# Attention exponentials read from PSUM with a bias, in a recurrent kernel whose four engines wait on one another

## The chip, the cores and the metric

The kernel runs on one core of a Trainium2 chip. The metric is the device time of one execution in microseconds, lower is better. The engines are called PE (TensorE), DVE (VectorE), ACT (ScalarE), POOL (GpSimd) and SP; each runs its own queue of instructions in order, and semaphores are the only thing that ties one queue to another.

## The reference, cut to what matters

An LSTM runs over 128 time steps of 16 sequences, its outputs go through a causal attention with 16 heads of 64 (keys and values from a 32-wide latent), the result is added to x and goes through a GRU of 128 steps, and a mixture of 8 experts (top 2) follows. The part that is changed is the softmax:

```python
attn = jnp.einsum('bqhd,bkhd->bhqk', q_blhd, k_blhd) / jnp.sqrt(HD)
attn = jax.nn.softmax(jnp.where(mask, attn, neg_inf), axis=-1)
y_blhd = jnp.einsum('bhqk,bkhd->bqhd', attn, v_blhd)
```

## The kernel before, in words

All stages are staggered over one loop of steps k. The LSTM's time step t = k runs in step k, the GRU's time step g = k - 29 in the same step, so that both recurrences advance once a step, and every engine has the same loop with its own part of the step written out by hand. Nothing is scheduled by a tool: the order in the code is the order in each queue.

The attention works on blocks of 16 queries. Write a step as k = 16q + o, where o is its offset in block q (1 to 8). Eight *units* belong to a block, one for each offset 2 to 9. A unit holds two sequences with 16 heads and 16 queries each, which makes four tiles of 128 rows; the keys are the L = 16q positions so far. For unit n:

- step of its scores (offset o): PE writes the four tiles, 128 x L each, into the single PSUM bank `pS` (`scores`, L493 to L500); DVE takes the row maxima `mx` (`maximum`, L858) and writes `P = pS - mx` for all four tiles in one instruction (`subtract`, L867). The bank is free for the next writer once `sub_done` has counted.
- next step: ACT takes the exponential of `P` in place, four tiles in one instruction (`exps`, L730), PE transposes the four tiles into `pV` (`turn_probs`, L507), ACT copies them out (L736).
- step after that: PE multiplies by the latents (`values`), DVE normalises (`normalise`, `turn_values`).

`P` has three buffers, `mx` has one. `pS` is also the bank into which the latents are projected every eighth step (`lat_q`).

Within a step the queues are, in order. PE: `g_step` (GRU gates), `l_step` (LSTM gates), `values`, `g_candidate` (the matmul of the GRU's candidate, pG<-gRZ), `lat_q` if due, `scores`, one expert's down projection (pY), `turn_probs`, then what is due of the router, the fills of pL and pG and the propagation. ACT: `gT` (tanh of the GRU's gates), `lT` (tanh of the LSTM's gates), `exps` of the unit before, `gC` (tanh of the candidate), `lC`, then the rest. DVE: `gRZ` (L949, releases `g_candidate`), the LSTM's cell, `normalise`, `gB`, `ghi`, `g`, then `glo` (L973, released to the next `g_step`), `hhi`, `hlo`, then `maximum`, `subtract`, at offset 6 the second half of a router's work (`route_rest`), the expert's accumulation `acc` (L940), `turn_values`, and at offset 5 the first half (`route_first`), which ends in `low`; ACT's `th` (L778) waits for `low` and stands ahead of the next step's `gT`.

The experts' Gelu (L746) runs at offsets 13 to 15, 0 and 1; from block 3 on this puts an `ACT_TABLE_LOAD` ahead of the first exponential of a block, at offset 3. It happens six times.

Of the kernel before, what the change touches and what calls it, by code (L numbers as in the profile page):

```python
# [15 lines left out]
NU = B // 2  # L16
# [8 lines left out]
O_S, O_T, O_V = 2, 3, 4  # L25
# [9 lines left out]
def unit_at(k, o):  # L35
    q, u = divmod(k - o, TB)
    return NU * (q - 1) + u if u < NU and 1 <= q <= NBLK else None
# [42 lines left out]
def build(nc, a, out):  # L80
# [3 lines left out]
    ALU = mybir.AluOpType  # L84
    ACT = mybir.ActivationFunctionType
    AX = mybir.AxisListType

    ctx = ExitStack()
    with ctx:
# [6 lines left out]
        def sem(name):  # L96
            return ctx.enter_context(nc.semaphore(name))
# [9 lines left out]
        bias = sb("bias", [128, 2, 128])  # L107
# [60 lines left out]
        mx = sb("mx", [128, 4])  # L168
        P = sb("P", [128, 3, 4, 128])
# [46 lines left out]
        cleared = sem("cleared")  # L216
# [49 lines left out]
        qbd_done = sem("qbd_done")  # L266
        s_mm = sem("s_mm")
        mx_done = sem("mx_done")
        sub_done = sem("sub_done")
        exp_done = sem("exp_done")  # L270
        pt_mm = sem("pt_mm")
        pt_done = sem("pt_done")
# [28 lines left out]
        NCLEAR = 10  # L301
        PARTS = (0, 64, 96)

        def S_of(L):
            return pS[:, :].rearrange("p (j t) -> p j t", j=4)[:, :, 0:L]

# [5 lines left out]
        def keys(p):  # L312
            return TB * (p + 1)
# [96 lines left out]
        def _(pe):  # L410
# [49 lines left out]
            def lat_q(G, k):  # L460
                hi, lo = (flat(t[:, GS * G + 1:GS * G + GS + 1, :]) for t in (hhi, hlo))
                pe.wait_ge(l_lo, GS * G + GS)
                if G == 0:
                    pe.wait_ge(set_kvd, 2)
                    pe.wait_ge(set_qk, 1)
                    pe.wait_ge(set_qklo, 1)
                if G:
                    pe.wait_ge(lat_done, G)
                before = len([j for j in range(k) if unit_at(j, O_S) is not None])
                if before:  # L470
                    pe.wait_ge(sub_done, before)
                mm(pS[:, 0:TOK], Wkvdhi[:, :], hi, start=True)
                mm(pS[:, 0:TOK], Wkvdhi[:, :], lo)
                mm(pS[:, 0:TOK], Wkvdlo[:, :], hi).then_inc(lat_mm, 1)
                before_c(k)
                for g in range(HG):
                    Y, heads = pC[:, TOK * g:TOK * (g + 1)], slice(128 * g, 128 * (g + 1))
                    mm(Y, Wqkhi[:, heads], hi, start=True)
                    mm(Y, Wqkhi[:, heads], lo)
                    last = mm(Y, Wqklo[:, heads], hi)  # L480
                last.then_inc(q_mm, 1)

            def scores(n, k):
                p, u = divmod(n, NU)
                L = keys(p)
                if n == 0:
                    pe.wait_ge(set_mask, 2)
                pe.wait_ge(lat_split, 2 * (2 * p + 2))
                pe.wait_ge(qbd_done, HQ * (n + 1))
                pe.wait_ge(lat_done, min(k // GS, NG))  # L490
                if n:
                    pe.wait_ge(sub_done, n)
                mm(S_of(L)[:, :, L - TB:L], ident16[:, :], cmask[:, :, :], start=True)  # L493
                for j in range(4):
                    b = 2 * u + j // 2
                    S = S_of(L)[:, j, :]
                    mm(S, flat(qbd[:, n % 2, 0, j, :, :]), lathi[:, b, 0:L])
                    mm(S, flat(qbd[:, n % 2, 0, j, :, :]), latlo[:, b, 0:L])
                    last = mm(S, flat(qbd[:, n % 2, 1, j, :, :]), lathi[:, b, 0:L])
                last.then_inc(s_mm, 1)  # L500

            def turn_probs(n):
                pe.wait_ge(exp_done, n + 1)
                if n:
                    pe.wait_ge(on_done, n)
                for j in range(4):
                    last = nc.tensor.transpose(pV[:, 128 * j:128 * (j + 1)], P[:, n % 3, j, :], ident[:, :])  # L507
                last.then_inc(pt_mm, 1)
# [148 lines left out]
        def _(act):  # L657
            A = nc.scalar.activation
# [67 lines left out]

            def exps(n):
                L = keys(n // NU)
                act.wait_ge(sub_done, n + 1)
                A(P[:, n % 3, :, 0:L], P[:, n % 3, :, 0:L], ACT.Exp).then_inc(exp_done, 1)  # L730

            def pt_copy(n):
                act.wait_ge(pt_mm, n + 1)
# [50 lines left out]
        def _(dve):  # L784
# [70 lines left out]

            def maximum(n):
                dve.wait_ge(s_mm, n + 1)
                V.tensor_reduce(mx[:, :], S_of(keys(n // NU)), AX.X, ALU.max).then_inc(mx_done, 1)  # L858

            def subtract(n):  # L860
                L = keys(n // NU)
                dve.wait_ge(mx_done, n + 1)
                if n >= 3:
                    dve.wait_ge(pt_mm, n - 2)
                if n == 0:
                    dve.wait_ge(cleared, NCLEAR)
                V.tensor_tensor(P[:, n % 3, :, 0:L], S_of(L), mx[:, :].unsqueeze(2).to_broadcast([128, 4, L]),  # L867
                                ALU.subtract).then_inc(sub_done, 1)

            def normalise(n):  # L870
                dve.wait_ge(o_mm, n + 1)
# [71 lines left out]
            for k in range(STEPS):  # L943
                t, g = k, k - LAG
                if 0 <= g < T:
                    at = T if g % 4 == 0 else g - 1
                    prev, last = g8[:, at, :], T + 1
                    dve.wait_ge(g_tanh, g + 1)
                    V.scalar_tensor_tensor(gRZ[:, :, :], gT[:, :, :], 1.0, g8[:, at:last + 1:last - at, :],  # L949
                                           ALU.add, ALU.mult).then_inc(g_rh, 1)  # L950
                    V.scalar_tensor_tensor(gA[:, :], gT[:, 1, :], -1.0, prev, ALU.add, ALU.mult).then_inc(g_a, 1)
                if t < T:
                    dve.wait_ge(l_tanh, t + 1)
                    V.scalar_tensor_tensor(lP[:, :, :], lT[:, 0:2, :], 1.0, lT[:, 3:5, :], ALU.add, ALU.mult).then_inc(l_mul, 1)
                    V.tensor_scalar(oK[:, :], lT[:, 2, :], SH / 2, SH / 2, ALU.mult, ALU.add)
                    dve.wait_ge(l_mul, t + 1)
                    V.scalar_tensor_tensor(lT[:, 4, :], lP[:, 1, :], 0.5, lP[:, 0, :], ALU.mult, ALU.add).then_inc(l_c, 1)
                if unit_at(k, O_V) is not None:
                    normalise(unit_at(k, O_V))
                if 0 <= g < T:  # L960
                    dve.wait_ge(g_c, g + 1)
                    V.tensor_tensor(gB[:, :], gRZ[:, 1, :], gC[:, :], ALU.mult).then_inc(g_b, 1)  # L962
                    dve.wait_ge(g_b, g + 1)
                    keep = -SH / 2 if g % 4 == 0 else -0.5
                    V.scalar_tensor_tensor(ghi[:, g, :], gA[:, :], keep, gB[:, :], ALU.mult, ALU.add).then_inc(g_hi, 1)  # L965
                    V.scalar_tensor_tensor(g8[:, g, :], gA[:, :], keep, gB[:, :], ALU.mult, ALU.add).then_inc(g_h, 1)
                if t < T:
                    dve.wait_ge(l_tc, t + 1)
                    V.tensor_tensor(hhi[:, t + 1, :], oK[:, :], lC[:, :], ALU.mult).then_inc(l_hi, 1)  # L969
                    V.tensor_tensor(hfull[:, :], oK[:, :], lC[:, :], ALU.mult).then_inc(l_h, 1)  # L970
                if 0 <= g < T:
                    dve.wait_ge(g_h, g + 1)
                    V.tensor_tensor(glo[:, g, :], g8[:, g, :], ghi[:, g, :], ALU.subtract).then_inc(g_lo, 1)  # L973
                if t < T:
                    dve.wait_ge(l_h, t + 1)
                    V.tensor_tensor(hlo[:, t + 1, :], hfull[:, :], hhi[:, t + 1, :], ALU.subtract).then_inc(l_lo, 1)
                setup(k)
                if half_at(k) is not None:
                    add_x(half_at(k))
                if k % GS == 0 and GS <= k <= T:  # L980
                    lat_copy(k // GS - 1)
                    q_rest(k // GS - 1)
                if k % TB == 1 and TB < k <= T + 1:
                    turn_latents(k // TB - 1)
                if unit_at(k, O_S) is not None:
                    maximum(unit_at(k, O_S))
                    subtract(unit_at(k, O_S))
                if route_at(k - 1) is not None:
                    route_rest(*route_at(k - 1))
                for down in down_at(k):  # L990
                    combine(*down)
                if unit_at(k, O_V) is not None:
                    turn_values(unit_at(k, O_V))
                if route_at(k) is not None:
                    route_first(*route_at(k))
# [51 lines left out]
```

## Time and profile before

| | |
|---|---|
| three runs | 729.1, 722.74, 728.73 us, median 728.73 |
| the profiled execution | 724.37 us, its span 722.6 us |
| PE busy | 623.3 us, 86% of the span |
| DVE busy | 420.9 us, 58% |
| ACT busy | 293.4 us, 41% |
| POOL busy | 134.3 us, 19% |
| mean granted clock of PE | 0.898 of full |
| block 3, block 5, block 7 (16 steps each) | 76.9, 78.1, 75.8 us |

Busy time is a sum over instructions; matmuls overlap one another and their ends are modelled. The traced time is one execution; the runs differ among themselves by 0.9%. In a timeline row the columns are start and length in us, engine, line, operation, output <- input, shape and count, and in square brackets how long the engine had been idle and who ended that. The span begins at the first instruction.

### The profile page before, as it was taken

How to read it: one execution, taken by the hardware profiler on the slowest of the kernel's cores; microseconds unless marked ns; L12 is line 12 of the kernel's file. 1: busy time of each engine (PE TensorE's matmuls, PEld its weight loads, DVE VectorE, ACT ScalarE, POOL GpSimd, SP SyncE). 2: the span in 40 equal slices, each digit the busy share in tenths (PEclk: the TensorE clock that was granted, in tenths of full speed). 3: DMA queues.
4: the chain of work that ended last, by engine and by line, in shares of the span. 5: the costliest groups of instructions: out<-in, count | busy, mean ns of one | idle time of the engine just before them, and what ended most of it. 6: DMA issues, size and time to landing. Idle time of an engine off the chain costs nothing.

```text
span 722.6 us, 18818 instructions
## 1 busy us (share of the span) xinstructions
PE 623.3 (86%) x6952; PEld 550.6 (76%) x6952; DVE 420.9 (58%) x2372; ACT 293.4 (41%) x1004; POOL 134.3 (19%) x339
## 2 busy tenths in 40 slices
PE   5988889988899888898898889888988888877898
PEld 2656767876788878887888778877888688766787
DVE  2476656664586558655776478655875476435321
ACT  1354323235532464245422653355434532451143
POOL 4006204200331024102320043003310231000000
PEclk8795785599988999999979999999999999998599
DMA  9400000000000000000000000000000000000000
GB/s 257 176 1 1 2 1 1 3 1 1 2 3 1 5 5 3 2 5 5 3 1 2 8 3 3 1 10 1 2 2 5 6 1 2 4 6 2 0 8 9
DMA packets 5528, 10.03 MB, mean 14 GB/s; under 512 B 1827, under 2 KB 4527, under 8 KB 5054
## 3 DMA queue, kind: packets, MB, share of 16 engines
q1 hardware_dynamic: 4686, 6.47, 2.5%
q10 hardware_dynamic: 752, 2.37, 1.3%
q8 instruction: 56, 0.92, 0.6%
q14 instruction: 34, 0.28, 0.1%
HBM read 7.79 MB, written 1.05 MB: 12 GB/s over the span
## 4 chain that ended last, share of the span: by engine, by line
PE 64%; DVE 18%; ACT 10%; issue 6%; DMA 1%; SPq 0%; POOL 0%; DVEq 0%; POOLq 0%
PE pY L412 18%; PE pG L412 11%; PE pH L412 10%; PE pV L412 8%; PE pL L412 6%; PE pV L507 4%; ACT hid L746 4%; PE pS L412 3%; PE pC L412 3%; ACT PTs L736 2%; DVE acc L940 1%; DMA lWx<-in_lWx 1%; DVE gRZ L949 1%; DVE ghi L965 1%; DVE mx L858 1%
## 5 line engine op out<-in xcount | busy, mean ns | idle before, releaser
L412 PE MATMUL pY<-w,hid 128*128 128x128 f32 x1024 | 155.3, 299 | 0.0
L412 PEld LDWEIGHTS pY<-w,hid 128*128 128x128 f32 x1024 | 136.3, 207 | 0.1
L746 ACT ACTIVATE hid<-pH,b 128x256 f32<-128x256 f32 x256 | 105.6, 471 | 63.0 <-PE pH L412 61.6
L385 POOL COPY qbd<-qh 32x256 f16<-32x256 f16 x256 | 104.3, 408 | 141.5 <-PE pS L412 127.8
L949 DVE SCALAR_TENSOR_TENSOR gRZ<-gT,g 128x32 f32<-128x32 f32 x128 | 26.8, 210 | 115.4 <-ACT gT L754 115.2
L412 PE MATMUL pG<-gRZ,gW 128*128 128x16 f32 x256 | 51.1, 276 | 36.5 <-DVE gRZ L949 36.4
L412 PE MATMUL pV<-latN,PTs 128*128 128x33 f32 x512 | 76.8, 298 | 6.6 <-ACT PTs L736 6.6
L736 ACT ACTIVATE PTs<-pV 128x512 f32<-128x512 f32 x64 | 38.2, 597 | 107.6 <-PE pV L507 107.6
L412 PEld LDWEIGHTS pG<-gRZ,gW 128*128 128x128 f32 x256 | 42.8, 210 | 46.1 <-DVE gRZ L949 45.3
L412 PEld LDWEIGHTS pV<-latN,PTs 128*128 128x128 f32 x512 | 70.1, 212 | 9.4 <-ACT PTs L736 8.6
L412 PE MATMUL pH<-ghi,w1hi 128*128 128x256 f16 x256 | 70.6, 276 | 6.6 <-ACT hid L746 5.5
L412 PE MATMUL pH<-glo,w1hi 128*128 128x256 f16 x256 | 70.8, 277 | 0.0
L412 PE MATMUL pH<-ghi,w1lo 128*128 128x256 f16 x256 | 70.7, 276 | 0.0
L940 DVE SCALAR_TENSOR_TENSOR acc<-pY,gates,acc 128x128 f32<-128x128 f32 x128 | 44.4, 347 | 33.6 <-PE pY L412 32.4
L962 DVE TENSOR_TENSOR gB<-gRZ,gC 128x16 f32<-128x16 f32 x128 | 24.2, 189 | 61.6 <-ACT gC L764 60.9
L764 ACT ACTIVATE gC<-pG 128x16 f32<-128x16 f32 x128 | 23.3, 182 | 81.8 <-PE pG L412 81.6
L754 ACT ACTIVATE gT<-pG 128x32 f32<-128x32 f32 x128 | 24.8, 194 | 70.5 <-PE pG L412 70.5
L412 PE MATMUL pY<-still 128*128 128x512 bf16 x138 | 48.8, 476 | 1.2 <-DVE still L786 1.2
L392 POOL TENSOR_TENSOR eq<-eq,tri 128x64 f32<-128x64 f32 x16 | 5.1, 318 | 238.1 <-DVE gt L904 238.1
L507 PE MATMUL pV<-ident,P 128*128 128x128 f32 x256 | 46.5, 312 | 2.5 <-DVE On L874 2.5
L412 PE MATMUL pL<-hhi,lWhi 128*128 128x16 f16 x512 | 41.8, 171 | 4.4 <-DVE hhi L969 4.4
L412 PEld LDWEIGHTS pL<-hhi,lWhi 128*128 128x128 f16 x512 | 35.2, 102 | 13.1 <-DVE hhi L969 11.0
(155 smaller groups left out, 1448.3 us busy)
## 6 DMA issues: line engine op xcount, KB each, us to landing
w<-in_w SPq DMA_DIRECT2D x2, 2048.0 KB, 10.8
out<-acc SPq DMA_DIRECT2D x16, 64.0 KB, 1.5
xT<-in_xT ACTq DMA_DIRECT2D x1, 960.0 KB, 10.4
hid<-in_WqT ACTq DMA_DIRECT2D x1, 512.0 KB, 5.6
hid<-in_Wout ACTq DMA_DIRECT2D x1, 512.0 KB, 7.9
lWh<-in_lWh SPq DMA_DIRECT2D x1, 256.0 KB, 2.8
lWx<-in_lWx SPq DMA_DIRECT2D x1, 256.0 KB, 9.5
gWh<-in_gWh SPq DMA_DIRECT2D x1, 192.0 KB, 7.5
```

Of the source, the lines that this page charges most:

```text
L385: pool.tensor_copy(qbd[r, n % 2, :, :, q, :], qh[r, p % 2, :, 2 * u:2 * u + 2, :, :].rearrange("p l b (g c) t -> p l (b g) (c t)", g=2)).t ...
L412: return nc.tensor.matmul(o, lhsT=lhsT, rhs=rhs, start=start, stop=stop, skip_group_check=True)
L507: last = nc.tensor.transpose(pV[:, 128 * j:128 * (j + 1)], P[:, n % 3, j, :], ident[:, :])
L736: A(PTs[:, n % 2, :, :].rearrange("p j q -> p (j q)"), pV[:, :], ACT.Copy).then_inc(pt_done, 1)
L746: A(hid[:, e % NHID, 2 * cp + c, :], pH[cp][:, 256 * c:256 * (c + 1)], ACT.Gelu, bias=b1[:, e, 2 * cp + c:2 * cp + c + 1], scale=1.0 / SP) ...
L754: A(gT[:, :, :], pG[:, 0:2, g % GS, :], ACT.Tanh, scale=1.0 / SP).then_inc(g_tanh, 1)
L764: A(gC[:, :], pG[:, 2, g % GS, :], ACT.Tanh, scale=1.0 / SP).then_inc(g_c, 1)
L858: V.tensor_reduce(mx[:, :], S_of(keys(n // NU)), AX.X, ALU.max).then_inc(mx_done, 1)
L940: V.scalar_tensor_tensor(acc[:, m % 3, tg, :], pY[:, D * tg:D * (tg + 1)], gates[:, m % 2, tg, e:e + 1], acc[:, m % 3, tg, :], ALU.mult, A ...
L949: V.scalar_tensor_tensor(gRZ[:, :, :], gT[:, :, :], 1.0, g8[:, at:last + 1:last - at, :], ALU.add, ALU.mult).then_inc(g_rh, 1)
L962: V.tensor_tensor(gB[:, :], gRZ[:, 1, :], gC[:, :], ALU.mult).then_inc(g_b, 1)
L965: V.scalar_tensor_tensor(ghi[:, g, :], gA[:, :], keep, gB[:, :], ALU.mult, ALU.add).then_inc(g_hi, 1)
```

## The change

The DVE subtraction is gone, and with it the semaphore `sub_done`. The reduction writes the negated maximum; ACT reads the scores from PSUM and adds that as a bias. A bias is one value per row, so each of the four tiles has an instruction of its own. Whoever waited for `sub_done` now waits for `exp_done`, which counts four per unit. For `scores(n)` and `lat_q` this means: before, the bank was free after DVE's work at the end of the step before; now it is free after ACT's work in the same step, behind `gT` and `lT`. `maximum(n)` has a new wait on the exponentials of the unit before, since these read the single `mx`.

```diff
                 if before:
-                    pe.wait_ge(sub_done, before)
+                    pe.wait_ge(exp_done, 4 * before)
                 mm(pS[:, 0:TOK], Wkvdhi[:, :], hi, start=True)
...
                 if n:
-                    pe.wait_ge(sub_done, n)
+                    pe.wait_ge(exp_done, 4 * n)
                 mm(S_of(L)[:, :, L - TB:L], ident16[:, :], cmask[:, :, :], start=True)
...
             def turn_probs(n):
-                pe.wait_ge(exp_done, n + 1)
+                pe.wait_ge(exp_done, 4 * (n + 1))
...
             def exps(n):
                 L = keys(n // NU)
-                act.wait_ge(sub_done, n + 1)
-                A(P[:, n % 3, :, 0:L], P[:, n % 3, :, 0:L], ACT.Exp).then_inc(exp_done, 1)
+                act.wait_ge(mx_done, n + 1)
+                if n == 0:
+                    act.wait_ge(cleared, NCLEAR)
+                if n >= 3:
+                    act.wait_ge(pt_mm, n - 2)
+                for j in range(4):
+                    A(P[:, n % 3, j, 0:L], S_of(L)[:, j, :], ACT.Exp, bias=mx[:, j:j + 1]).then_inc(exp_done, 1)
...
             def maximum(n):
                 dve.wait_ge(s_mm, n + 1)
-                V.tensor_reduce(mx[:, :], S_of(keys(n // NU)), AX.X, ALU.max).then_inc(mx_done, 1)
-
-            def subtract(n):
-                L = keys(n // NU)
-                dve.wait_ge(mx_done, n + 1)
-                if n >= 3:
-                    dve.wait_ge(pt_mm, n - 2)
-                if n == 0:
-                    dve.wait_ge(cleared, NCLEAR)
-                V.tensor_tensor(P[:, n % 3, :, 0:L], S_of(L), mx[:, :].unsqueeze(2).to_broadcast([128, 4, L]),
-                                ALU.subtract).then_inc(sub_done, 1)
+                if n:
+                    dve.wait_ge(exp_done, 4 * n)
+                V.tensor_reduce(mx[:, :], S_of(keys(n // NU)), AX.X, ALU.max, negate=True).then_inc(mx_done, 1)
```

ACT's queue at offset 3 of block 3, the first step with a table load, up to the next step's exponentials. Before:

```order
L754 ACTIVATE gT<-pG 128x32 [waits g_rz]
L757 ACTIVATE lT<-pL 128x64 [waits l_gates]
L730 ACT_TABLE_LOAD
L730 ACTIVATE P<-P 128x4x48 [waits sub_done]
L764 ACTIVATE gC<-pG 128x16 [waits g_cand]
L767 ACTIVATE lC<-lT 128x16 [waits l_c]
L736 ACTIVATE PTs<-pV 128x512 [waits o_mm,pt_mm]
```

And now (lines up to the definition of `exps` have moved by one, those behind it by four):

```order
L758 ACTIVATE gT<-pG 128x32 [waits g_rz]
L761 ACTIVATE lT<-pL 128x64 [waits l_gates]
L734 ACT_TABLE_LOAD [waits pt_mm]
L734 ACTIVATE P<-pS,mx 128x48 [waits mx_done]
L734 ACTIVATE P<-pS,mx 128x48 x3
L768 ACTIVATE gC<-pG 128x16 [waits g_cand]
L771 ACTIVATE lC<-lT 128x16 [waits l_c]
L740 ACTIVATE PTs<-pV 128x512 [waits o_mm,pt_mm]
```

One exponential has become four in the same place, between `lT` and `gC`; the load stands where it stood, with a wait on transposes of an older unit.

PE's queue in that step, from the candidate's matmul to the next step's GRU gates, as it stands before:

```order
L412 MATMUL pS<-cmask,ident 128x4x16 [waits lat_done,sub_done,qbd_done,lat_split]
L412 MATMUL pS<-lathi,qbd 128x48
...
L412 MATMUL pY<-b2P,onesP 128x128 [waits acc_done,gelu]
L412 MATMUL pY<-w,hid 128x128 x4
L507 MATMUL pV<-ident,P 128x128 [waits on_done,exp_done]
...
L412 MATMUL pG<-glo,gWhi 128x16 [waits g_lo]
```

And now:

```order
L411 MATMUL pS<-cmask,ident 128x4x16 [waits lat_done,exp_done,qbd_done,lat_split]
L411 MATMUL pS<-lathi,qbd 128x48
...
L411 MATMUL pY<-b2P,onesP 128x128 [waits acc_done,gelu]
L411 MATMUL pY<-w,hid 128x128 x4
L506 MATMUL pV<-ident,P 128x128 [waits on_done,exp_done]
...
L411 MATMUL pG<-glo,gWhi 128x16 [waits g_lo]
```

No matmul has moved; the wait at the head of the scores is on ACT's work of the same step, and the expert's matmuls, the transposes and the next step's gates are queued behind it.

## Rows read from the trace of the kernel before

**Rows 1.** The page: busy time by engine; the chain that ended last.

```profile
PE 623.3 (86%) x6952; PEld 550.6 (76%) x6952; DVE 420.9 (58%) x2372; ACT 293.4 (41%) x1004; POOL 134.3 (19%) x339
PE 64%; DVE 18%; ACT 10%; issue 6%; DMA 1%; SPq 0%; POOL 0%; DVEq 0%; POOLq 0%
```

**Rows 2.** Groups by line and form: busy us, mean ns of one | idle before.

```profile
L746 ACT ACTIVATE hid<-pH,b 128x256 f32<-128x256 f32 x256 | 105.6, 471 | 63.0 <-PE pH L412 61.6
...
L724 ACT ACTIVATE qh<-pC 128x512 f16<-128x512 f32 x16 | 9.6, 597 | 6.2 <-PE pC L412 6.2
...
L730 ACT ACTIVATE P<-P 128x512 f32<-128x512 f32 x8 | 5.0, 627 | 0.7 <-DVE P L867 0.7
...
L730 ACT ACTIVATE P<-P 128x64 f32<-128x64 f32 x8 | 2.0, 249 | 0.4 <-DVE P L867 0.4
```

**Rows 3.** Timeline of ACT: a pair of Gelus behind one another, merged.

```profile
407.93 0.84 ACT L746 ACTIVATE hid<-pH,b 128x256 f32<-128x256 f32 x2
```

**Rows 4.** Timeline, block 3 offset 3, first step with a table load.

```profile
196.15 1.28 ACT L730 ACT_TABLE_LOAD   x1
196.47 0.40 PE L412 MATMUL pG<-gRZ,gW 128*128 128x16 f32 x2 [0.59 <-DVE gRZ L949]
196.71 0.19 PE L412 MATMUL pS<-cmask,ident 128*128 128x64 bf16 x1
197.72 0.17 ACT L764 ACTIVATE gC<-pG 128x16 f32<-128x16 f32 x1
198.56 0.17 PE L412 MATMUL pG<-ghi,gWlo 128*128 128x16 f16 x1
199.22 0.21 PE L412 MATMUL pG<-glo,gWhi 128*128 128x16 f16 x2 [0.50 <-DVE glo L973]
```

**Rows 5.** Timeline, block 8 offset 3, last step with a table load.

```profile
580.78 1.28 ACT L730 ACT_TABLE_LOAD   x1
581.69 0.19 PE L412 MATMUL pS<-cmask,ident 128*128 128x64 bf16 x1
583.90 0.17 PE L412 MATMUL pG<-ghi,gWlo 128*128 128x16 f16 x1
584.06 0.21 PE L412 MATMUL pG<-glo,gWhi 128*128 128x16 f16 x2
```

**Rows 6.** Timeline, block 2 offset 3, where no table is loaded.

```profile
118.70 0.23 ACT L757 ACTIVATE lT<-pL 128x64 f32<-128x64 f32 x1
119.50 0.21 PE L412 MATMUL pS<-cmask,ident 128*128 128x64 bf16 x1
```

**Rows 7.** Timeline, block 4 offset 4, a step with values ahead of the scores.

```profile
276.89 0.22 ACT L757 ACTIVATE lT<-pL 128x64 f32<-128x64 f32 x1
277.83 0.19 PE L412 MATMUL pS<-cmask,ident 128*128 128x64 bf16 x1
```

**Rows 8.** Timeline, block 6: from offset 5's subtraction to offset 6's scores.

```profile
440.02 0.56 DVE L867 TENSOR_TENSOR P<-pS,mx 128x384 f32<-128x384 f32 x1
441.81 0.21 ACT L778 ACTIVATE th<-low 128x8 f32<-128x8 f32 x1 [1.22 <-DVE low L906]
442.00 0.21 ACT L757 ACTIVATE lT<-pL 128x64 f32<-128x64 f32 x1
442.52 0.40 PE L412 MATMUL pG<-gRZ,gW 128*128 128x16 f32 x2 [0.80 <-DVE gRZ L949]
442.77 0.19 PE L412 MATMUL pS<-cmask,ident 128*128 128x64 bf16 x1
```

**Rows 9.** Timeline of PE, offset 7: the candidate's matmul in blocks 4 and 8.

```profile
292.54 0.40 PE L412 MATMUL pG<-gRZ,gW 128*128 128x16 f32 x2 [1.19 <-DVE gRZ L949]
600.66 0.61 PE L412 MATMUL pG<-gRZ,gW 128*128 128x16 f32 x2 [0.84 <-DVE gRZ L949]
```

**Rows 10.** Windows: length, busy by engine, granted PE clock; blocks 5, 7, one stretch.

```profile
335.60:413.70 78.10, 69.37 (x849) 64.74 (x846) 50.00 (x293) 34.67 (x122) 15.40 (x40) 0.93 0.01 3
491.70:567.50 75.80, 66.04 (x839) 61.07 (x836) 51.22 (x293) 35.50 (x123) 15.41 (x40) 1.00 0.01 4
...
426.00:429.40 3.40, 2.36 (x45) 2.25 (x43) 2.54 (x12) 2.40 (x6) 1.54 (x5) 1.00 0.02 5
```

More of the change, by code:

```diff
@@ L268, in build @@
         mx_done = sem("mx_done")
-        sub_done = sem("sub_done")
         exp_done = sem("exp_done")
@@ L986, in _ @@
                     maximum(unit_at(k, O_S))
-                    subtract(unit_at(k, O_S))
                 if route_at(k - 1) is not None:
```

## The prediction

> **What bounds the kernel now.** I read the busy times and the chain of work first, then the groups by form, and then the timeline of all engines step by step, because no engine bounds the whole. PE is busy 86% of the span, and the chain passes 64% through PE, 18% through DVE and 10% through ACT [rows 1]: in most steps PE's queue is full, in a few it waits for the others. The reader should see which steps these are. At offset 3 (table load), offset 6 and, in three blocks, offset 7, PE stands idle before the candidate's matmul until DVE's `gRZ` is there: 0.59, 0.80, 1.19 and 0.84 us [rows 4, 8, 9]. There DVE's queue is late, and the subtraction is in it. Elsewhere `values` keeps PE busy, and DVE's subtraction costs nothing.
>
> **What goes.** 64 subtractions, 0.56 us each at 96 keys per tile [rows 8]. They are worth something only at the steps just named.
>
> **What comes: four exponentials per unit.** Before, one takes 249 ns at 64 columns and 627 at 512 [rows 2], so a column costs 378/448 = 0.844 ns. The nearest row to the new form is the Gelu, which reads PSUM, has a bias from SBUF, and takes 471 ns at 256 columns [rows 2]; a pair back to back takes 0.84, so the second starts 0.10 before the first ends [rows 3]. I take the new exponential as 471 - 0.844 x (256 - L). Four behind one another: 4 x that - 0.30. That is 0.88 us at L = 48, 1.04 at 96, 1.15 at 128; before it was 0.63 at the 128 end. Bounds: from below the copy out of PSUM, 597 ns at 512 columns [rows 2], 165 without its columns against 255 for the Gelu: four are 0.36 us cheaper. From above no overlap at all: 0.30 dearer. The Gelu row is nearest in source and bias, so I take it. The reduction with negation and its extra wait I put at nothing: that wait is met before the scores it reads exist.
>
> The Trainium skill (ScalarE: Activation LUTs, "What ACT_TABLE_LOAD costs") gives an ACTIVATE with a bias pointer as 280 + 0.833 N ns with 93 ns of overlap. The Gelu row is 5% below it. By the page four at 96 columns are 1.16 us instead of 1.04; with 0.12 more at each step that ends in the exponentials the result would be about 1.5 us above mine.
>
> **Where they lie on PE's path.** The scores of a step now wait for the exponentials of the same step. A hand-over from ACT to PE I take at 0.05 us.
>
> *Offset 3, six blocks with a table load.* Block 3: the load ends at 197.43, exponentials may end at 198.33, scores start at 198.38 in place of 196.71: 1.67 later [rows 4]. Expert, transposes and next gates are queued behind. The `glo` matmuls started at 199.22 after a wait; without it they would have followed the last `ghi` matmul at 198.67 [rows 4], so 0.55 is absorbed and 1.12 stays. The gain on `gRZ` is lost here, since the scores wait longer for ACT. Block 8: load ends at 582.06, exponentials at 583.23, scores at 583.28 for 581.69, 1.59 later; 584.06 was 0.13 behind 583.93 [rows 5], so 1.46 stays. The four blocks between, read alike, give 1.04, 1.19, 1.10 and 1.40. Sum 7.3 us.
>
> *Offset 3 without a load, two blocks.* Exponentials start 0.10 before `lT` ends, at 118.83, and take 0.83 at L = 32: scores at 119.71 for 119.50 [rows 6]. Twice 0.2: 0.4 us.
>
> *Offset 4.* Block 4, L = 64: start 277.01, four take 0.93, scores at 277.99 for 277.83 [rows 7], 0.16 late; similar in block 3, nothing in the later ones, whose step has more ahead. 0.3 us. At offset 5 the scores come 0.1 to 0.4 late too, but the next step waits on DVE's chain from `gC`, which is not moved; that absorbs it. At 7 to 9 other work covers the four.
>
> *Offset 6, a gain.* `th` waits for DVE's `low`, and stands ahead of `gT` and `lT` [rows 8]. Without the subtraction all of it comes 0.56 earlier in block 6: `lT` ends at 441.65, exponentials start at 441.55, end at 442.59, scores at 442.64 for 442.77 [rows 8]. 0.13 gained; the rest of 0.56 is eaten by the three further exponentials. Six blocks: -0.8 us.
>
> *Offset 7, a gain.* Three blocks (4, 7, 8) wait for DVE here, 1.19 in block 4 and 0.84 in block 8 [rows 9], behind a chain that had the subtraction of two steps. Both gone, most of the idle time goes, but 0.13 was already counted. About 0.85 in each: -2.5 us.
>
> **Sum.** 7.3 + 0.4 + 0.3 - 0.8 - 2.5 = +4.7 us. The profiled execution took 724.4, so this gives 729.1, 0.65% more. The median of the runs is 728.7, which would give 733.4. I forecast 731, between the two.
>
> **Rivals.**
>
> *PE's clock falls in the longer idle times.* PE gets a second pause in each table step. For it: block 5 had a mean clock of 0.93 and took 78.1 us, block 7 with clock 1.00 took 75.8, although it has more keys [rows 10]. Against it: the stretch at block 6's table step has PE busy only 2.36 of 3.40 us and the clock stays at 1.00, which is the 2.4 GHz level [rows 10]. Price: 2.3 a block in four or five blocks more, +10, so 739. Slower. Chance 0.19.
>
> *The exponentials don't overlap* (ends on the slower side). If the bias or the PSUM read keeps ACT from starting the next one early, each unit costs 0.30 more: table steps +1.8, offset 4 now late in all six blocks +1.6, offset 3 elsewhere +0.6, offset 6 +1.9, and `gC` becomes late at offsets 5 and 8, some +2.5. 737.5. It decides from four taking over about 1.2 us at 96 columns. Against it: pairs with bias do overlap [rows 3]. Chance 0.07.
>
> *The exponentials are cheap*, at the lower bound: table steps -2.2, offset 3 elsewhere -0.4, offset 4 -0.3, offset 6 -2.1: 724.1, no change. The columns speak for it, the Gelu row against. Chance 0.12.
>
> *The change does nothing on the path.* PE is the busiest engine and everything here is hidden; 724.4. Against it: a table step leaves the exponentials behind scores that PE has already started [rows 4, 5]. Chance 0.05.
>
> *Faster.* The falls of the clock that block 5 shows [rows 10] go away because DVE is less late (-6 over the blocks), and the exponentials are cheap: 718. Needs both. Chance 0.07.
>
> *My forecast*, 729 to 733: chance 0.5.
>
> **How the numbers follow.** A change of 1% is about what can be told from none. My forecast lies 0.65% up; the runs' own spread is 0.9%, so I give a fifth of its 0.5 to slower. Slower: 0.10 + 0.19 + 0.07 = 0.36, I say 0.35. Faster 0.07. Same 0.58. The range runs from the cheap exponentials on a quick run to the falling clock: 721 to 740; outside are the faster case and about half of the clock's. The likeliest case's own range is 726 to 736.
>
> **What the profile after would show.** (a) Rows of ACT with 128x128 in, 128x128 out near 0.36 us, and four merged at 1.15; at 96 columns 1.04. (b) At offset 3 of blocks 3 to 8, `pS<-cmask` idle before it, released by ACT, and starting 1.4 to 1.7 later against the load than before. (c) At offset 6 `th` about half a microsecond sooner after the maximum, and the wait for `gRZ` shorter. (d) At offset 7 of blocks 4, 7, 8 the idle time before `pG<-gRZ` nearly gone. (e) No wait of `maximum` on ACT. I am wrong if the scores also wait at offsets 7 to 9, if PE catches up after the table step elsewhere, or if the granted clock differs between the traces.

## The result: 3% slower, and the profile after

The changed kernel took 751.15 us (median of four executions, 748.17 to 765.98), the kernel before 728.91. The ratio is 1.030, 95% interval 1.021 to 1.039. The intervals here leave out executions in which the clock was disturbed; the table further down takes all. I had forecast 731, within 721 to 740, and "no change" as the likeliest. The time lies outside the range, and it went to the side that I gave 0.35.

The page of the profiled execution (750.85 us): busy time, the span in 40 slices, the granted clock of PE in tenths.

```profile
span 749.1 us, 19009 instructions
PE 642.6 (86%) x6952; PEld 569.1 (76%) x6952; DVE 392.3 (52%) x2308; ACT 323.6 (43%) x1196; POOL 133.8 (18%) x339
PEclk8795585599989998689989998999999999997599
PE 68%; DVE 13%; ACT 12%; issue 5%; DMA 1%; SPq 0%; POOL 0%; DVEq 0%; POOLq 0%
```

Against [rows 1] DVE has lost its 29 us of subtraction and ACT has gained 30 us. PE is busy 19 us longer with the same 6952 matmuls: that alone says that they ran slower, and the mean granted clock is 0.872 for 0.898.

What PE waits for, all of the span, after (us in total, times, longest):

```profile
PE pG L411 <- DVE gRZ L945: 28.1, 51, 1.5
PE pS L411 <- ACT P L734: 16.2, 20, 2.2
```

The same view of before:

```profile
PE pG L412 <- DVE gRZ L949: 36.4, 56, 1.5
```

The change did what it says: 8 us less waiting for DVE. In exchange there are 16 us of waiting for the exponentials, of which there was none. 11.3 of them lie at offset 3 of blocks 3 to 8; the scores also wait at offset 6 of the same six blocks (0.21 to 0.42 us each, 1.9 in all), at offset 5 of four blocks (0.9), at offset 8 of three (0.6) and once in block 1 (1.4).

Timeline of the changed kernel at offset 3 of block 6, ACT, then PE:

```profile
446.53 0.22 ACT L761 ACTIVATE lT<-pL 128x64 f32<-128x64 f32 x1
446.78 1.28 ACT L734 ACT_TABLE_LOAD   x1
448.07 1.04 ACT L734 ACTIVATE P<-pS,mx 128x96 f32<-128x96 f32 x4
...
447.04 0.40 PE L411 MATMUL pG<-gRZ,gW 128*128 128x16 f32 x2 [0.54 <-DVE gRZ L945]
...
449.25 0.21 PE L411 MATMUL pS<-cmask,ident 128*128 128x64 bf16 x1 [1.82 <-ACT P L734]
450.22 0.31 PE L411 MATMUL pY<-b2P,onesP 128*128 128x128 bf16 x1
450.32 1.92 PE L411 MATMUL pY<-w,hid 128*128 128x128 f32 x8
```

And PE in the same place before:

```profile
428.42 0.19 PE L412 MATMUL pS<-cmask,ident 128*128 128x64 bf16 x1
428.95 0.22 PE L412 MATMUL pY<-b2P,onesP 128*128 128x128 bf16 x1
429.01 1.11 PE L412 MATMUL pY<-w,hid 128*128 128x128 f32 x8
```

The four exponentials take 1.04 us, as forecast to the second digit. The scores start when they end. But then the scores take 0.97 us up to the expert instead of 0.53, and the expert's eight entries 1.92 instead of 1.11: the matmuls behind the wait run at half speed. The granted clock says the same. Windows of PE, changed kernel, six stretches that end about where the wait at offset 3 ends (blocks 3 to 8; length, PE busy, granted clock):

```profile
200.60:204.00 3.40, 1.18 (x25) 0.83 0.00 0
280.80:284.20 3.40, 1.18 (x22) 1.00 0.03 10
366.20:369.60 3.40, 1.09 (x25) 1.00 0.01 2
445.80:449.20 3.40, 1.09 (x23) 0.91 0.01 2
525.00:528.40 3.40, 0.99 (x23) 1.00 0.00 0
602.60:606.00 3.40, 0.96 (x14) 0.94 0.00 0
```

And the stretches right behind them:

```profile
204.00:207.40 3.40, 3.40 (x35) 0.50 0.00 0
284.20:287.60 3.40, 3.37 (x39) 0.58 0.00 0
369.60:373.00 3.40, 3.40 (x39) 0.57 0.00 0
449.20:452.60 3.40, 3.35 (x30) 0.59 0.00 0
528.40:531.80 3.40, 3.15 (x49) 1.00 0.02 5
606.00:609.40 3.40, 3.40 (x26) 0.56 0.00 0
```

In all six PE was busy for only 1.0 to 1.2 of 3.4 us, and in five of them it then ran mostly at 1.2 GHz instead of 2.4 (in block 7, with PE busy 0.99, it stayed at full clock). In the kernel before PE was busy 2.36 of 3.40 around block 6's table step [rows 10], and the stretch behind was at full clock:

```profile
428.40:431.80 3.40, 3.31 (x51) 1.00 0.00 0
```

**Where the 26.5 us of span went.** From the starts of `gT` in the two traces, step by step (each step runs from one `gT` to the next; us):

| | before | changed | more |
|---|---|---|---|
| up to the start of block 3 | 182.5 | 187.9 | 5.4 |
| offset 3, blocks 3 to 8 (six steps) | 24.1 | 40.2 | 16.1 |
| other steps of blocks 3 to 8 | 434.1 | 438.2 | 4.1 |
| behind block 8 | 81.8 | 82.7 | 0.9 |

Windows of blocks 4 and 7 after, for [rows 10] (the fields are the same; the last but two is the clock):

```profile
268.20:353.50 85.30, 75.34 (x851) 70.36 (x848) 45.88 (x285) 38.22 (x147) 15.34 (x40) 0.86 0.01 3
512.10:590.00 77.90, 67.54 (x839) 62.53 (x835) 47.31 (x285) 39.15 (x146) 15.35 (x40) 0.98 0.01 3
```

Block 4 took 76.2 us before and 85.3 now; block 7 75.8 and 77.9. The worst block is the one with the lowest clock.

### The profile page after: what moved, and what is told of

Its sections match the earlier page's. It is cut to its first block, busy times and chain, and to the rows that moved or that the text cites. A ratio compares the mean times of both kernels' runs of the same rounds, so it can differ in the third digit from the quotient of the medians.

```text
span 749.1 us, 19009 instructions
## 1 busy us (share of the span) xinstructions
PE 642.6 (86%) x6952; PEld 569.1 (76%) x6952; DVE 392.3 (52%) x2308; ACT 323.6 (43%) x1196; POOL 133.8 (18%) x339
## 3 DMA queue, kind: packets, MB, share of 16 engines
HBM read 7.79 MB, written 1.05 MB: 12 GB/s over the span
## 4 chain that ended last, share of the span: by engine, by line
PE 68%; DVE 13%; ACT 12%; issue 5%; DMA 1%; SPq 0%; POOL 0%; DVEq 0%; POOLq 0%
PE pY L411 21%; PE pG L411 10%; PE pH L411 9%; PE pV L411 8%; PE pL L411 6%; PE pV L506 5%; PE pS L411 5%; ACT hid L750 3%; PE pC L411 3%; ACT PTs L740 3%; ACT P L734 2%; DMA lWx<-in_lWx 1%; ACT L734 1%; DVE gRZ L945 1%; DVE acc L936 1%
## 5 line engine op out<-in xcount | busy, mean ns | idle before, releaser
L411 PE MATMUL pY<-w,hid 128*128 128x128 f32 x1024 | 164.3, 311 | 0.0
L411 PEld LDWEIGHTS pY<-w,hid 128*128 128x128 f32 x1024 | 144.6, 218 | 0.1
L734 ACT ACTIVATE P<-pS,mx 128x16 f32<-128x16 f32 (+7 forms) x256 | 61.3, 333 | 0.3 <-DVE mx L864 0.2
L506 PE MATMUL pV<-ident,P 128*128 128x128 f32 x256 | 50.7, 334 | 2.5 <-DVE On L870 2.5
```

Source lines behind the costliest of these rows:

```text
L411: return nc.tensor.matmul(o, lhsT=lhsT, rhs=rhs, start=start, stop=stop, skip_group_check=True)
L734: A(P[:, n % 3, j, 0:L], S_of(L)[:, j, :], ACT.Exp, bias=mx[:, j:j + 1]).then_inc(exp_done, 1)
```

## How the runs are read: time against slow-clock time

Executions of one kernel differ by several per cent here, and each comes with a span S and a mean granted clock c. With two levels, 1.0 and 0.5, the time at the lower one is 2(1 - c)S. Over 60 executions of the kernel before (59 taken beside the experiments, and the profiled one), S = 669.8 + 0.364 x slow-clock time, correlation 0.96: 716.5 us at clock 0.907 (133 us slow), 741.5 at 0.862 (205 us slow). So every kernel is described by two numbers: its *base*, the mean span brought to 150 us of slow clock with that slope, and the median of its *slow-clock time*. The slope is that of a whole execution. Slow clock in a place where PE's queue is full costs up to 0.5 per us, so a base that differs from another by a few us may still hold some clock. With a slope of 0.5 in place of 0.364 the changed kernel's base would be 6 us above that of the kernel before and not 11: the sum of the two parts is firmer than how it is split.

| kernel | executions | median time | slow-clock time | base |
|---|---|---|---|---|
| before | 60 | 732.1 | 162 | 724.4 ± 0.2 |
| changed (first runs and e5) | 10 | 755.1 | 197 | 735.3 ± 0.5 |
| e1 before, moved wait alone | 4 | 753.7 | 195 | 735.7 ± 0.9 |
| e2 changed, wait filled with matmuls | 4 | 746.7 | 179 | 734.4 ± 0.5 |
| e3, e9 changed, early table load | 22 | 729.7 | 157 | 725.2 ± 0.2 |
| e4 changed, expert first | 4 | 742.3 | 183 | 728.7 ± 0.2 |
| e6 before, early table load | 12 | 732.0 | 167 | 723.5 ± 0.3 |
| e7 changed, one exponential | 4 | 745.7 | 184 | 730.1 ± 0.7 |
| e8, e10 changed, early load and expert first | 24 | 729.0 | 164 | 722.6 ± 0.2 |

(± is the standard error of the mean.) Changed against before: 35 us more slow clock x 0.364 = 13 us, and 11 us of base; the medians differ by 23. None of the 10 executions of the changed kernel had less than 185 us of slow clock, while half of those of the kernel before had less than 162. It is not chance of single executions.

## The experiments

Two theories. STALL: the time lost is PE's longer wait at offset 3, and the clock is the same lottery for both kernels. CLOCK: the wait also makes PE's clock fall behind it. I used them as rivals with numbers in each expectation.

**e1: the moved wait alone, in the kernel before.** The subtraction and the single exponential stay; only who releases `pS` changes.

```diff
                 if before:
-                    pe.wait_ge(sub_done, before)
+                    pe.wait_ge(exp_done, before)
...
                 if n:
-                    pe.wait_ge(sub_done, n)
+                    pe.wait_ge(exp_done, n)
```

> The kernel before, with its subtraction and its single exponential, but the scores and the latents' projection wait for the exponential instead of the subtraction. It has the moved wait alone. At offset 3 of blocks 3 to 8 the scores should start about 1.0 to 1.4 us later (load end plus 0.4 to 0.6 us). Theory STALL (time lost is only the stall that is not absorbed): +4 to +6 us on the kernel before. Theory CLOCK (the stall makes PE run at its lower level for a stretch behind it): six slow stretches right behind the six stalls, +10 to +18 us, mean granted clock near 0.88.

Measured: 753.7 us, ratio 1.034 (1.018 to 1.049). All of the loss is there, without a single new exponential: base and slow-clock time (735.7 and 195) are those of the changed kernel (735.3 and 197) within their errors. Its offset 3 in block 6:

```profile
432.52 0.40 PE L412 MATMUL pG<-gRZ,gW 128*128 128x16 f32 x2 [0.80 <-DVE gRZ L949]
433.96 0.21 PE L412 MATMUL pS<-cmask,ident 128*128 128x64 bf16 x1 [1.05 <-ACT P L730]
434.93 0.31 PE L412 MATMUL pY<-b2P,onesP 128*128 128x128 bf16 x1
435.04 2.02 PE L412 MATMUL pY<-w,hid 128*128 128x128 f32 x8
```

Two waits of 0.80 and 1.05 us close together, and the expert at half speed behind them. The slow stretch follows all six table steps of this trace. Against the 60 executions of the kernel before it is 22 us slower, more than CLOCK had said (10 to 18).

**e2: PE's wait filled.** Seven 128x512 matmuls, written to a bank that nobody reads, ahead of the scores at offset 3.

```diff
+                    n = unit_at(k, O_S)
+                    if n % NU == 1 and n // NU >= 2:
+                        pe.wait_ge(on_done, n - 1)
+                        for _ in range(7):
+                            mm(pV[:, :], still[:, 0:128], still[:, :], start=True)
                     scores(unit_at(k, O_S), k)
```

> The changed kernel with seven extra 128x512 bf16 matmuls on PE ahead of the scores at offset 3 of blocks 3 to 8, written to a bank that nobody reads; they fill about 1.5 us of the 1.8 us for which PE stood idle, and add no work behind it. STALL: no gain, 749 to 753. CLOCK: the slow stretch behind the six stalls goes, 736 to 742, mean granted clock above 0.885.

Measured: 746.7 us, ratio 1.024 (1.009 to 1.040). Timeline and two windows behind one another at offset 3 of block 6 (of the seven matmuls six are on record there):

```profile
439.75 1.46 PE L411 MATMUL pV<-still 128*128 128x512 bf16 x6
441.83 0.19 PE L411 MATMUL pS<-cmask,ident 128*128 128x64 bf16 x1 [0.63 <-ACT P L739]
442.37 0.22 PE L411 MATMUL pY<-b2P,onesP 128*128 128x128 bf16 x1
442.42 1.11 PE L411 MATMUL pY<-w,hid 128*128 128x128 f32 x8
```

```profile
438.80:442.20 3.40, 2.50 (x29) 1.00 0.01 2
442.20:445.60 3.40, 3.15 (x48) 1.00 0.00 0
```

The scores start as late as in the changed kernel (3.02 us behind `gT`'s start in both), but PE was busy 2.50 of 3.40, and the expert takes 1.11 again. This is the cleanest pair of the study: same wait for the data, other clock behind it. None of its six table steps has the slow stretch. They last 5.32, 5.42, 5.56, 5.69, 5.82 and 5.62 us, 33.4 in all, against 40.2 in the changed kernel and 24.1 before. So of the 16.1 us at offset 3, 9.3 are the wait and 6.8 the clock. Block 7 of the changed kernel, the one whose clock did not fall, took 5.82 us as well. As a forecast of the whole time the expectation was a miss: CLOCK wanted 736 to 742, STALL 749 to 753, and the median lies between. Slow-clock time fell by 18 us in the median only; in the trace offset 5 of five blocks lasted 6.3 to 6.8 us for 4.7 to 5.3 in the kernel before, and slow clock was in it, so part of it came back one or two steps later. Why there stays open.

**e3 (and e9): the table load out of the wait.** A one-column exponential of a spare tile at the end of ACT's offset 2, where ACT idles for 1.40 us; the load goes with it.

```diff
+        spare = sb("spare", [128, 1])
...
             act.wait_ge(cleared, 5)
+            act.wait_ge(set_hi, 3)
...
                 for up in ups:
                     activate(*up)
+                if k % TB == 2 and 3 <= k // TB <= NBLK:
+                    A(spare[:, :], h0T[:, 0:1], ACT.Exp)
```

> The changed kernel with a one-column exponential on a spare tile at the end of ACT's offset 2 in blocks 3 to 8, so that the table load (1.28 us) falls into ACT's idle time there. The scores at offset 3 should then wait for about 1.04 us of exponentials only, some 0.6 us in place of 1.8. STALL: 7 us less than the changed kernel, 743. CLOCK: the slow stretches go as well, 730 to 736, at or near the kernel before.

Measured: 728.9 us, ratio 0.990 (0.981 to 0.998). Offset 3 of block 6:

```profile
435.29 1.03 ACT L736 ACTIVATE P<-pS,mx 128x96 f32<-128x96 f32 x4
...
435.67 0.39 PE L412 MATMUL pG<-gRZ,gW 128*128 128x16 f32 x2 [0.54 <-DVE gRZ L949]
436.46 0.19 PE L412 MATMUL pS<-cmask,ident 128*128 128x64 bf16 x1 [0.40 <-ACT P L736]
```

The wait is 0.40 us in place of 1.82, and no table step has the slow stretch. Base 10 us lower, slow-clock time 40 us lower. That is just under the 730 to 736 of CLOCK and far from the 743 of STALL. One instruction of a column takes back all of the loss but about 1 us of base. (The wait on `set_hi` stands in the setup; e8 and e10 below do without it.)

> The changed kernel with the early table load, unedited from its first run, for a second set of executions on one chip. CLOCK: base about 1 us above the kernel before at equal slow-clock time, slow-clock time about the same as the kernel before's (median near 160 us), so 0 to 1 us above it. The first set's ratio of 0.990 would then have been luck with the clock. STALL makes no other statement here.

Measured: 730.3 us, ratio 1.005 (0.997 to 1.013). The gain over the kernel before in the first set did not come again: the base is 0.8 above it over both sets, and three of the first ten executions had only 126 us of slow clock.

**e4: useful work in the wait.** The expert's down projection ahead of the scores at offset 3 (`expert_down` is called before `scores` there; nothing else moves).

> The changed kernel with the expert's down projection (1.17 us of matmuls) ahead of the scores on PE at offset 3 of blocks 3 to 8, so that useful work covers the wait. STALL: the six stalls shrink from 1.8 to about 0.7 us and that is all, 744. CLOCK: PE idles too little for the fall, 732 to 738.

Measured: 742.3 us (724.3 to 747.3, too scattered for a ratio), base 728.7, 6.6 below the changed kernel, slow-clock time 183. The base went as wanted, the slow clock by only 14 of the 35 us; in its trace no table step is slow but the step behind it is, in blocks 3 and 6. My 732 to 738 was too low, and 742.3 is nearer to the 744 of STALL. Four executions do not settle more.

**e5: the changed kernel again**, so that its clock could be judged on more executions.

> The changed kernel once more, unedited, beside the others of this set on one chip, so that each execution's time can be set against its mean granted clock. Theory CLOCK: time = a base at equal slow-clock time plus about 0.42 us for every us at the lower level, where the base is 7 to 9 us above that of the kernel before and the slow-clock time has a median some 25 to 40 us above it; in all 17 to 24 us slower. Theory STALL (the clock is chance and the same for both): the slow-clock times of the two have the same median, and the difference is 7 to 9 us.

Measured: 755.7 us, ratio 1.035 (1.029 to 1.041). In this trace the slow stretch follows all six table steps. With the first trace that is 11 of 12; STALL, for which the slow-clock times should have been equal, is out (197 against 162). Of the numbers of CLOCK the slow-clock time came (35 us more, 25 to 40 expected), while the base lies 11 above the kernel before and not 7 to 9 (with the slope of 0.42 that I had then, it would be 9).

**e6: the early load in the kernel before**, the control for e3.

> The kernel before with the one-column exponential at the end of ACT's offset 2 in blocks 3 to 8, which moves the table load alone. In the kernel before nothing on PE waited for the load; it only held back the candidate's tanh, and with it the glo matmuls at offset 3, by 0.1 to 0.5 us. Both theories: base 1 to 2 us below the kernel before; slow-clock time unchanged. If its gain is 5 us or more, the gain of the changed kernel with the early load (about 7 us of base) is a gain of the load's place and not of the stall taken away.

Measured: 732.0 us, ratio 1.001 (0.997 to 1.006), base 0.9 lower. The load's place is worth 1 us of base by itself and 10 us once PE waits behind it.

**e7: one exponential instead of four.** It leaves out the subtraction of the maximum and scales the scores down; all four tiles in one instruction from PSUM.

> The changed kernel with one exponential per unit over all four tiles, read from PSUM, without the maximum as bias (it leaves out the subtraction of the maximum, the scores are scaled down to keep the exponentials finite). One instruction of 0.5 us at 96 columns in place of four of 1.04. STALL and CLOCK: the wait at offset 3 shrinks from 1.8 to about 1.3 us and steps at offset 6 gain 0.3; base 4 to 5 us below the changed kernel, 727 to 728 at 150 us of slow clock. CLOCK: the remaining stall still brings slow stretches behind most table steps, slow-clock time near the changed kernel's.

Measured: 745.7 us, base 730.1, that is 5.2 below the changed kernel (4 to 5 expected), slow stretches behind five of six table steps. Set beside e1, which has the same moved wait and one exponential but also the subtraction: 735.7 against 730.1. So leaving out the subtraction is worth about 5.6 us (± 1.2) and splitting the exponential costs about 5.2 (± 0.9). The first number also holds what reading from PSUM and the new wait of `maximum` are worth, which differ between e1 and e7 too. Those two, the purpose and the price of the change, cancel within their errors, and what is left is the moved wait.

**e8 (and e10): early load and expert first together.**

> The changed kernel with the table load at the end of offset 2 and the expert's down projection ahead of the scores at offset 3, blocks 3 to 8. Nothing should wait for the exponentials at offset 3 any more. Both theories: base 2 us below the changed kernel with the early load alone, 722 to 724 at 150 us of slow clock, level with or 1 us below the kernel before; CLOCK: slow-clock time like that of the kernel before.

Measured: 728.7 us, ratio 0.997 (0.992 to 1.002); the base is 722.3, within the 722 to 724 expected and 2.1 below the kernel before; over both sets it is 1.8 below.

> The changed kernel with the early load and the expert ahead of the scores at offset 3, unedited, for a second set of executions. Base 2 us below the kernel before at equal slow-clock time; CLOCK: slow-clock time near 160 us, so about 2 us (0.3%) faster than the kernel before.

Measured: 730.1 us, ratio 0.9986 (0.9951 to 1.0022). It is level with the kernel before; a gain of 0.2% is what the bases say, and neither set can tell it from none. No version beats the kernel before clearly.

## Why the prediction was wrong, by its own steps

- *The exponential's price*: right. 379 ns mean at 128 columns, 280 at 16, 1.04 us for four at 96:

```profile
L734 ACT ACTIVATE P<-pS,mx 128x128 f32<-128x128 f32 x32 | 9.1, 379 | 0.0
L734 ACT ACTIVATE P<-pS,mx 128x16 f32<-128x16 f32 x32 | 6.1, 280 | 0.2 <-DVE mx L864 0.2
```

  I had 363 and 268. They overlap, so that rival is out. The page ScalarE: Activation LUTs of the Trainium skill ("What ACT_TABLE_LOAD costs") would give 387 and 293 for a biased ACTIVATE of that size; single instructions lie between it and my numbers from the Gelu row, but four together were 1.04 us, not its 1.16.

- *Offset 3 with a table load, +7.3*: right mechanism, wrong size. The wait itself costs 9.3 (e2's six steps). Two terms were off. The hand-over from ACT's last exponential to the scores is 0.14 us (449.11 to 449.25), not 0.05. And what I took as absorbed by the wait for `glo`, 0.55 us in block 3, was not what counts: in e2's block 3 the `glo` matmuls start 1.12 us later behind the step's `gT` than before, exactly my number (4.73 for 3.61 us), but the next `gT` comes 1.47 later. It stands on ACT behind the copy `PTs` of the transposes, and these are queued on PE behind the late scores and the expert. ACT in block 6, before and in the changed kernel:

```profile
430.59 0.60 ACT L736 ACTIVATE PTs<-pV 128x512 f32<-128x512 f32 x1 [1.20 <-PE pV L507]
431.09 0.19 ACT L754 ACTIVATE gT<-pG 128x32 f32<-128x32 f32 x1
```

```profile
452.72 0.60 ACT L740 ACTIVATE PTs<-pV 128x512 f32<-128x512 f32 x1 [3.43 <-PE pV L506]
453.21 0.19 ACT L758 ACTIVATE gT<-pG 128x32 f32<-128x32 f32 x1
```

  From block 5 on `gT` followed that copy without idle time in the kernel before already, so there nothing was absorbed; in blocks 3 and 4 it was 0.3 us each. Over six steps the scores of e2 come 9.9 us later behind `gT`, 0.6 is absorbed, and 9.3 stays. (The 198.67 in the sum for block 3 was itself 0.08 too late: by the rule used for block 8, 0.03 behind the last row of `ghi`, it is 198.59.) With the clock behind it the six steps cost 16.1.

- *The step that failed: "PE's clock falls in the longer idle times", chance 0.19.* I named the mechanism and its time was +10, but I argued it down from a stretch with PE busy 2.36 of 3.40 us at full clock [rows 10]. That row is of the kernel before. I had just worked out that the change takes another 1.4 us of PE's work out of that same stretch, which leaves about 1.0 of 3.4 (1.04 is what the trace shows ahead of the scores in block 6), and did not put this number beside the row. It happened in 11 of 12 table steps. The price was a little low too: 35 us more of slow clock are 13 us over an execution, by the slope, for my 10. In the sum itself this term stood at nothing.

- *Offset 6, -0.8*: wrong in sign. I let `th` come 0.56 us earlier because the subtraction was gone. But DVE, freed of it, now waits for the expert's and the router's matmuls of PE at offset 5, and in block 6 `th` comes only 0.29 us sooner behind the `gT` of offset 5 (4.93 for 5.22). DVE there in the changed kernel:

```profile
461.07 0.55 DVE L864 TENSOR_REDUCE mx<-pS 128x4 f32<-128x384 f32 x1
462.00 0.35 DVE L936 SCALAR_TENSOR_TENSOR acc<-pY,gates,acc 128x128 f32<-128x128 f32 x1 [0.37 <-PE pY L411]
462.72 0.17 DVE L892 COPY lg<-pC 128x8 f32<-128x8 f32 x1 [0.15 <-PE pC L567]
```

  And then the scores of offset 6 wait for ACT in all six blocks. Block 4, before (`gT` at 286.76) and in e5's trace (`gT` at 301.05):

```profile
287.60 0.19 PE L412 MATMUL pS<-cmask,ident 128*128 128x64 bf16 x1
```

```profile
302.30 0.19 PE L411 MATMUL pS<-cmask,ident 128*128 128x64 bf16 x1 [0.26 <-ACT P L734]
```

  Offset 6 of block 4 takes 3.76 us in e5 and 3.35 before, offset 5 takes 4.77 and 5.01, all at full clock: together 0.17 longer, where I had 0.13 shorter. Of the 5.2 us that splitting costs by e7, 3.3 lie at offset 3, where e7's scores start 0.55 us earlier behind `gT` in each of the six blocks; those I had in the 7.3.

- *Offset 7, -2.5*: open. PE's waits for `gRZ` there fall from 4.5 us to 1.4, but too many of these steps run at the lower clock in one trace or the other to tell what the step gained.

- *The 731, put between 729.1 and 733.4*: the sum was made against one execution with clock 0.898, which is 147 us of slow clock. It was one of the better ones; the median over 60 is 162 us, and 732.1 us of time. That has no part in the 22 us by which the two kernels differ.

- *What would show it*: (a) and (e) came as written, (b) with 1.45 to 1.75 us. Of (c) the wait for `gRZ` at offset 6 did get shorter (5.0 us to 2.2 in all), but `th` did not come sooner after the maximum: 1.97 us behind its end in block 6 for 1.82 before. Of (d) the waits show the direction. Two of the three signs of being wrong also came: the granted clock differs, and the scores wait at offset 8 in blocks 5 to 7. The latter cost nothing in blocks 6 and 7, where offset 8 runs at full clock in both traces: 6.50 and 6.58 us for 6.51 and 6.58.

## What to carry to other kernels

When a wait is moved from one engine to another, look at what else stands in front of the new releaser in its queue. Here a table load of 1.28 us cost 1 us of base as long as nobody waited behind it and 10 us once PE did; one dummy activation in the idle time ahead restores that. And when a change makes TensorE idle, write down how busy it will be in the few microseconds around, not only how long it waits: the matmuls behind the wait may cost as much as the wait. Merging operations with a bias looks free on the engine that loses one; here four small instructions for one large cost about 5.2 us, and the subtraction that they made unnecessary was worth 5.6, the same within the errors.

## What the runs showed of the hardware that I had not expected

- A pause of 1.8 to 2.2 us, with PE busy 1.0 to 1.2 of 3.4 us, was followed by a stretch at 1.2 GHz in 11 of 12 cases (the changed kernel and e5). In e1 and e7 the pauses were shorter, 0.9 to 1.7 us, and the stretch followed in 11 of 12 as well. With the pause filled (e2, 2.50 of 3.40 busy in block 6) it followed in none of six, and in none of six in the kernel before, where it was 2.36 there.
- Filling the pause does not take the slow stretch away for good: e2 kept 179 us of slow clock, with falls at offset 5 in place of offset 3.
- One and the same kernel had between 133 and 205 us of slow-clock time, with spans of 716.5 and 741.5 us at the two ends; the correlation of the two is 0.96. Here the granted clock goes with most of the spread of the executions.
